# Adjacency visits of a graph kernel: three blocks take turns, and one operation marks the source rows of three visits

## What is computed

```python
def gnn_layer(x, W, b, src, dst):
    h = x @ W.T + b
    return relu(segment_sum(h[src], dst, num_segments=1250))

xn  = layernorm(x)
gnn = gnn_layer(gnn_layer(xn, W1, b1, src, dst), W2, b2, src, dst)
q, k, v = xn @ Wq.T, xn @ Wk.T, xn @ Wv.T
q = softmax(q, axis=-1) * 512 ** -0.5
k = softmax(k, axis=-2)                   # over the nodes
a = q @ (k.T @ v) + xn
x = x + gnn + (a @ M1.T @ M2.T + a)
x = x + moe(layernorm(x))                 # 8 experts, sinkhorn gates, 156 rows each
```

## Time and profile before

| | |
|---|---|
| median of 3 runs | 468.15 us (467.83 to 469.38) |
| the profiled execution | 468.61 us, of which 466.8 us are the span of its instructions |
| PE busy | 451.0 us, 97% of the span |
| DVE busy | 320.9 us, 69% |
| ACT busy | 150.6 us, 32% |
| granted clock of TensorE | 0.999 |
| stretch with visits (86 to 241 us) | PE busy all of it, DVE about nine tenths |

### The profile page before, as it was taken

One profiled execution on the slowest core, in us unless ns is written; L12 is line 12 of the kernel. 1 busy time (PEld: TensorE's weight loads), 2 busy tenths in 40 slices (PEclk: granted clock), 3 DMA queues, 4 the chain that ended last, 5 costly groups with the idle time before them and its releaser, 6 DMA issues.

```text
span 466.8 us, 6816 instructions
## 1 busy us (share of the span) xinstructions
PE 451.0 (97%) x2424; PEld 360.6 (77%) x2424; DVE 320.9 (69%) x1104; ACT 150.6 (32%) x272; POOL 63.1 (14%) x90
## 2 busy tenths in 40 slices
PE   7999999999999999999999999999999998878995
PEld 3788778888888888888779999877777776655783
DVE  6995699899998988897752110444645666777972
ACT  4686453322323332332222110222133114551110
POOL 4088200000000000000004000002300000006642
PEclk9999999999999999999999999999999999999999
DMA  8902002911000000001200000002744449305891
GB/s 219 287 1 91 1 0 91 219 50 65 2 1 1 1 1 1 1 2 20 108 0 4 1 1 1 1 0 53 277 139 134 134 142 380 131 1 190 289 356 71
DMA packets 20846, 40.46 MB, mean 87 GB/s; under 512 B 2953, under 2 KB 3283, under 8 KB 20805
## 3 DMA queue, kind: packets, MB, share of 16 engines
q1 hardware_dynamic: 18549, 32.55, 22.4%
q0 software_dynamic: 2256, 7.39, 4.5%
HBM read 30.10 MB, written 10.31 MB: 87 GB/s over the span
## 4 chain that ended last, share of the span: by engine, by line
PE 86%; DVE 8%; ACT 2%; issue 1%; DMA 1%; SPq 0%; POOLq 0%; DVEq 0%
PE ps L736 46%; PE ps L1031 9%; PE ps L957 9%; PE ps L848 5%; PE ps L723 5%; PE ps L1167 2%; ACT scrap_a L1424 1%; PE ps L1048 1%; PE ps L1137 1%; DMA X<-in_x 1%; PE ps L880 1%; PE ps L770 1%; PE ps L984 1%; PE ps L1008 1%; PE ps L1078 1%
## 5 line engine op out<-in xcount | busy, mean ns | idle before, releaser
L1713 DVE TENSOR_SCALAR RING_D<-places,PLACES 125x170 bf16<-125x170 f16 (+1 forms) x239 | 63.5, 266 | 0.0
L1714 DVE TENSOR_SCALAR RING_S<-iota,HOME 125x128 bf16<-125x128 f16 x239 | 60.4, 253 | 0.0
L957 PE MATMUL ps<-AT,H1H 125*128 125x416 f32 (+1 forms) x108 | 38.0, 352 | 0.0
L957 PE MATMUL ps<-AT,H1L 125*128 125x416 f32 (+1 forms) x108 | 38.0, 351 | 0.0
L1031 PE MATMUL ps<-H2H,AT 125*125 125x512 f32 x90 | 36.1, 402 | 0.0
L1031 PE MATMUL ps<-H2L,AT 125*125 125x512 f32 x90 | 35.5, 394 | 0.0
L1048 PE MATMUL ps<-WE0H 128*128 128x512 f32 x129 | 35.4, 408 | 0.0
L1781 DVE TENSOR_TENSOR ps<-ps,bias 125x512 f32<-125x512 f32 x20 | 14.0, 700 | 27.9 <-PE ps L736 27.9
L1860 DVE SCALAR_TENSOR_TENSOR ZL<-ps,ZH 128x416 fp32r<-128x416 f32 (+1 forms) x12 | 6.3, 585 | 38.7 <-ACT ZH L1369 38.7
L723 PEld LDWEIGHTS ps<-RING_D,RING_S 125*125 125x125 bf16 x239 | 25.7, 136 | 7.9
L605 POOL TENSOR_TENSOR G2L<-RAW_G,G2H 128x512 fp32r<-128x512 f32 x4 | 5.0, 1287 | 192.2 <-ACT G2H L1186 192.2
(11 more groups left out here) (410 smaller groups left out, 1171.7 us busy)
## 6 DMA issues: line engine op xcount, KB each, us to landing
RAW_E<-in_experts SPq DMA_DIRECT2D x8, 1024.0 KB, 9.9
RAW_AGAIN<-in_experts SPq DMA_DIRECT2D x3, 1024.0 KB
X<-in_x SPq DMA_DIRECT2D x1, 2240.0 KB
out_x<-X SPq DMA_DIRECT2D x10, 224.0 KB
scratch<-X SPq DMA_DIRECT2D x10, 224.0 KB
scratch<-Y SPq DMA_DIRECT2D x10, 224.0 KB
RAW_K<-in_WkT SPq DMA_DIRECT2D x4, 256.0 KB, 4.2
RAW<-in_mW2T SPq DMA_DIRECT2D x1, 1024.0 KB, 11.8
```

Source lines behind the costliest of these rows:

```text
L957: pe.matmul(place(f), h[0:TT, k, 128 * f:128 * (f + 1)], AT[0:TT, k, c0:c1], start=(k == 0 and n == 0), stop=False)
L1713: V.tensor_scalar(hot_d(v, width(b)), places[0:ET, 0:width(b)], PLACES[0:ET, c:c + 1], None, ALU.is_equal)
L1714: V.tensor_scalar(hot_s(v), iota[0:ET, :], HOME[0:ET, c:c + 1], None, ALU.is_equal).then_inc(done["marked"], 1)
```

## The change

The visits are regrouped in 104 **sets**: the 20 visits of block 0 in sets of up to 3, and then, inside a group, the visit number s of each of its blocks (block 0 apart) side by side. 87 sets hold 3 visits, 13 hold 2, 4 hold 1. For a set DVE still makes `hot_d` visit by visit, but all its `hot_s` in one operation: an equality of `iotas` (128 x 3, the row number written three times) with `HOME` of the set's visits, repeated over the 128 rows. The result is interleaved, so the weights of one visit lie 3 elements (6 bytes) apart. `HOME` becomes fp16. `marked` and `visited` count sets. Ring A holds 2 sets, ring B 9 sets. In PSUM a group is opened once, by its first matmul, and closed by its last.

The places change too: the places in vp and cp take one set each, `q{i}` has one place instead of two (2 sets), and `x{i}` has two, at 0 and 12, instead of four (3 sets each); 54 places in all. DVE's calls of `mark_next` are moved to match.

```diff
-RING_A, RING_B = 6, 16
+RING_A, RING_B = 2, 9
...
+    sets = [[(0, s) for s in range(o, min(o + SIDE, VISITS[0]))] for o in range(0, VISITS[0], SIDE)]
+    for g in range(NG):
+        blocks = range(max(SIDE * g, 1), min(SIDE * (g + 1), NB))
+        for s in range(VISITS[blocks[0]]):
+            sets.append([(b, s) for b in blocks if s < VISITS[b]])
...
-    spots = [("vp0", 6, 3)]
+    spots = [("vp0", 6, 1)]
     for u in ("vp1", "vp2", "vp3", "cp0", "cp1", "cp2", "cp3"):
-        spots += [(u, n, 3) for n in (0, 6)]
+        spots += [(u, n, 1) for n in (0, 6)]
     for i in range(NT + 1):
         if i < NT:
-            spots += [(f"q{i}", 0, 4), (f"q{i}", 6, 4 if i % 4 == 1 else 3)]
+            spots += [(f"q{i}", 0, 2)]
         if i:
-            spots += [(f"x{i - 1}", n, 3 if n == 12 else 4) for n in (0, 6, 12, 18)]
-    spots += [(f"h{i}", 6, 3) for i in range(NT)]
+            spots += [(f"x{i - 1}", n, 3) for n in (0, 12)]
+    spots += [(f"h{i}", 6, 1) for i in range(NT)]
...
-            link(nc.gpsimd.iota(iota[:], [[1, 128]], base=0, channel_multiplier=0,
+            link(nc.gpsimd.iota(iotas[:], [[1, 128], [0, SIDE]], base=0, channel_multiplier=0,
...
-                    pe.matmul(PS[4 + g % 2][0:TT, o:o + width(b)], hot_s(v)[:, 0:TT], hot_d(v, width(b)), start=(s == 0),
-                              stop=(s == VISITS[b] - 1), skip_group_check=True).then_inc(done["visited"], 1)
+                    for k, (b, s) in enumerate(SETS[v]):
+                        o = NT * (EDGES[b] - EDGES[SIDE * g])
+                        mm = pe.matmul(PS[4 + g % 2][0:TT, o:o + width(b)], hot_s(v)[:, 0:TT, k], hot_d(v)[:, k, 0:width(b)], start=(k == 0 and (b, s) == (SIDE * g, 0)),
+                                       stop=(v in GROUP_ENDS and k == len(SETS[v]) - 1), skip_group_check=True)
+                    mm.then_inc(done["visited"], 1)
...
-                        V.tensor_scalar(hot_d(v, width(b)), places[0:ET, 0:width(b)], PLACES[0:ET, c:c + 1], None, ALU.is_equal)
-                        V.tensor_scalar(hot_s(v), iota[0:ET, :], HOME[0:ET, c:c + 1], None, ALU.is_equal).then_inc(done["marked"], 1)
+                        for k, (b, _) in enumerate(SETS[v]):
+                            V.tensor_scalar(hot_d(v)[:, k, 0:width(b)], places[0:ET, 0:width(b)], PLACES[0:ET, c + k:c + k + 1], None, ALU.is_equal)
+                        V.tensor_tensor(hot_s(v)[:, :, 0:m], iotas[0:ET, :, 0:m], HOME[0:ET, c:c + m].unsqueeze(1).broadcast_to([ET, 128, m]),
+                                        ALU.is_equal).then_inc(done["marked"], 1)
...
             for c in range(C):
                 context_left(c)
-                mark_next(2)
+                mark_next((2, 2, 1, 2)[c])
             for i in range(NT + 1):
-                if i < NT and i:
+                if i:
                     mark_next()
                 if i >= 2:
                     add_mix(i - 2)
-                if i < NT and i:
-                    mark_next()
                 if i < NT:
                     q_peak(i)
                 if i:
-                    mark_next()
                     q_left(i - 1)
                     mark_next()
                 if i < NT:
                     q_inverse(i)
-                if i:
-                    mark_next()
+                if i and i < NT:
                     mark_next()
```

More of the change, by code:

```diff
@@ L188, with mark_sets @@
 EDGES, COLUMN = block_columns()
-ORDER = [(b, s) for b in range(NB) for s in range(VISITS[b])]
+def mark_sets():
+    sets = [[(0, s) for s in range(o, min(o + SIDE, VISITS[0]))] for o in range(0, VISITS[0], SIDE)]
[3 more added lines that the diff above has]
+            sets.append([(b, s) for b in blocks if s < VISITS[b]])
+    assert sum(map(len, sets)) == NV
+    for one in sets:
+        assert [COLUMN[x] for x in one] == list(range(COLUMN[one[0]], COLUMN[one[0]] + len(one)))
+    return sets
+SETS = mark_sets()
+NS = len(SETS)
+GROUP_ENDS = {v: SETS[v][0][0] // SIDE for v in range(NS) if v == NS - 1 or SETS[v + 1][0][0] // SIDE > SETS[v][0][0] // SIDE}
 def visits_in_products():
-    spots = [("vp0", 6, 3)]
+    spots = [("vp0", 6, 1)]
     for u in ("vp1", "vp2", "vp3", "cp0", "cp1", "cp2", "cp3"):
-        spots += [(u, n, 3) for n in (0, 6)]
+        spots += [(u, n, 1) for n in (0, 6)]
     for i in range(NT + 1):
         if i < NT:
-            spots += [(f"q{i}", 0, 4), (f"q{i}", 6, 4 if i % 4 == 1 else 3)]
+            spots += [(f"q{i}", 0, 2)]
         if i:
-            spots += [(f"x{i - 1}", n, 3 if n == 12 else 4) for n in (0, 6, 12, 18)]
-    spots += [(f"h{i}", 6, 3) for i in range(NT)]
+            spots += [(f"x{i - 1}", n, 3) for n in (0, 12)]
+    spots += [(f"h{i}", 6, 1) for i in range(NT)]
     found, v = [], 0
     for unit, n, count in spots:
-        count = min(count, NV - v)
+        count = min(count, NS - v)
         if count:
@@ L322, in gps_block @@
         tri = small("tri", [128, 128], F32, "a")
[L323 removed]
         places = small("places", [128, HOTW], F16, "a")
[L325 removed]
+        HOME = small("HOME", [128, NV], F16, "a")
         PLACES = small("PLACES", [128, NV], F32, "a")
@@ L346, in gps_block @@
         rsum = small("rsum", [128, 2, NT], F32, "a")
-        kmt = small("kmt", [128, C], F32, "a")
+        kmt = small("kmt", [128, C], F32, "k")
         krs = small("krs", [128, 2, C], F32, "a")
@@ L713, in visits @@
                 for v in VISITS_AT.get((unit, n), ()):
-                    b, s = ORDER[v]
-                    g = b // SIDE
-                    if s == 0 and b % SIDE == 0:
+                    g = SETS[v][0][0] // SIDE
+                    if SETS[v][0] == (SIDE * g, 0):
                         if g < 2:
```

41 lines of the change are left out of this document (22 added, 19 removed).

## The result

The changed kernel takes 472.34 us (median of 6 runs, 471.85 to 474.36) against 468.10 before (6 runs, 467.83 to 469.67): ratio 1.0086, 95% interval 1.0065 to 1.0107. It is slower by 4.2 us; the prediction said about 471.6 and "slower".

A forecast was written before the change was run, and what follows sets the result against it. PE sets the pace, DVE's savings alone are worth nothing. Transposes +0.82, moved visits +1.17, fewer places -1.03, loads +2.52 sum to +3.5 us: 472.1 profiled, about 471.6 median; whole range 467.3 to 476.5.

The forecast's parts named there:

- (a): PE's places for visits: 83 become 54, each costing 0.038 us of its own, so -1.1 us.
- (b): PE's weight loads in visits: 6-byte steps take 85 ns, +12 ns for each visit behind a visit, 2.8 us in all.
- one stream at 8.8 bytes/ns: Visits' weight load on PE: rate taken from the product's 512 fp32 columns, giving 85 ns for 750 bytes.
- the small prices of the earlier trace: PE loads of 128 weights: 0.046 us at 12-byte steps, 0.035 at 8; held perhaps not to carry over to 125.
- the load stays hidden: Rival for PE's visit loads: spaced weights cost nothing, +0.7 us, 468.9, no measurable difference; chance 0.27.
- as slow as fp32's: Rival for PE's visit loads: 107 ns each, 476.7 us in all; chance 0.08.
- (c): DVE's merged equality of 384 elements: 357 ns long, 0.265 us of DVE's time, a set of three 0.785.
- one element per cycle: Rival for DVE's set operation: 0.2 us more per set, +1.0 us on everything, 472.6 or 469.9; chance 0.10.
- (d): PE at tile 0's transposes: five sets in front of q_peak(0) delay the softmax, a wait of about 1.7 us.
- No other wait over 0.3 us in the stretch: PE in the stretch of the visits: besides 1 to 2 us idle once at L904, no wait above 0.3 us.
- disappears in the same wait: First visit of q1 on PE: perhaps 0.1 us late, absorbed by the wait at tile 0's transposes.

The follow-up runs named there:

- e9: Kernel before, on PE alone: the four places of each x run as two, visits of 0 in front of 6, 12 of 18; 468.30 us, ratio 1.0003.
- e1: Changed kernel with each home marked by itself into dense weights, sets, places and calls kept; 472.16 us, ratio 1.0083 to the kernel before.
- e2: Changed kernel with the three sets of the first place of x0 marked behind tile 0's softmax; 471.07 us, ratio 1.0062 to the kernel before.
- e7: Changed kernel with x0's first three sets marked behind tile 0's softmax, 128 weights a visit, two sets in h0; 469.43 us, ratio 1.0034.
- e11: e9 plus, in q2 to q9, the visits of place 0 run in front of matmul 6; 468.25 us, ratio 0.9994 to the kernel before.
- e12: e11 with DVE taking q_left(0) and q_left(9) one place earlier; 468.14 us against 468.88 for the kernel before, ratio 0.9987.
- b1: Changed kernel with rows of equal matmuls on PE and comparisons on DVE added to measure rates, results unused; 500.97 us in a single run.
- e8: Kernel before with 128 dense weights a visit instead of 125, nothing else; 469.53 us against 467.87, ratio 1.0041.

## Why the prediction was right, and where it was off

The forecast, about 471.6, stands 0.7 us below the measured 472.3, and the terms that make it up are the ones found; one is missing (below).

**(a) Fewer places.** Predicted 29 x 0.038 = 1.1 us. e9 gives 31 ns a place, so 0.9 us. The reason given, the next fp32 load that a visit is too short to hide, is what PE's loads show: the two fp32 loads behind a row of visits start 0.11 us apart (108 ns unrounded), the loads of visits 76, which is 32 ns more. In the kernel before, behind the four visits at 131.41:

```profile
131.63 0.19 PEld L736 LDWEIGHTS ps<-MPH,XTH 128*125 128x125 f32 x1
131.74 0.19 PEld L736 LDWEIGHTS ps<-MPL,XTH 128*125 128x125 f32 x1
```

The 38 were too much for two reasons. A visit behind a visit costs 75 ns, not 73 (by e1 and e9: 0.493 - 0.233 - 3 x 0.075 is 0.035). And the first visit of a row starts 229 ns behind the product's matmul, where the next matmul would start after 233, 4 ns that a count from the first visit on leaves out.

**(b) Weights 6 bytes apart.** Predicted 85 ns, measured 86.7 in the visits and 86 to 87.5 by itself. Against dense rows of the same length in e1, a row of nine is 0.090 longer, one of six 0.055, of three 0.018; over the 54 rows 2.6 us. The choice of "one stream at 8.8 bytes/ns" over the small prices of the earlier trace rows was the step that decided the sign, and half of it was luck. That those small prices don't carry over held: they are of 128 weights, which at 6 bytes take 33 ns or less. But the 8.8 bytes/ns came from a stream of columns, and the stream that was seen at both clocks hangs on the clock (170 columns: 144 ns at 0.50, 75 at 1.00), while the load doesn't. So the two are not the same thing, and that their rates are alike at a granted clock of 1.00 is luck as far as the runs show. The rival "the load stays hidden" is refuted, and so is "as slow as fp32's".

**(c) DVE's operation.** This is a mis-sized term: 0.357 us predicted and 0.265 of DVE's time; measured 0.423 and 0.334 (113.59 to 113.92). I took 0.5 ns an element from rows of 6 and 4, where pairs come out even; a row of three costs two pair steps. The rival "one element per cycle" (0.2 more) is wrong too; the truth is a third of the way.

**(d) The wait.** Predicted at the transposes of tile 0, 1.7 us; it is there and is 1.8. DVE's maximum came at 117.34, not 116.86: 5 x 0.07 of that is term (c), and 0.14 is that the five sets began at 113.07, not 112.93. e2 shows the mechanism by removing it: moving three sets behind the softmax takes the wait away and 1.7 us with it. `q1`'s first sets were late by 0.27 us (a row of six in 1.05 instead of 0.77), named at 0.1. "No other wait over 0.3 us in the stretch" held. That the small wait "disappears in the same wait" held as long as the large one stood; in e2, which has no large one, the late sets of `q1` count.

**Missed.** The places shift the last set from `h7` to `h8`, and PE loses 0.32 us between `h9` and the first matmul on `AT`. The prediction has no term for it: it counts the place, and not what waits behind the last group. e7 shows that it goes away when the last set stands in `h7` again.

The ledger in AT time: loads +2.6, wait at the transposes +1.8, wait in `q1` +0.3, last group +0.3, places -0.9: +4.1, measured +4.2. The prediction's was +3.5: the missing 0.7 are for the most part (c)'s 0.36 and the last group's 0.32; the smaller misses of (a), (b) and `q1` nearly cancel.

## What to carry to other kernels

When an operation on an engine with spare time is merged, look first at what its new output layout does to the engine that reads it: here 12 us less work on DVE bought nothing, and 6-byte steps in 125 bf16 weights cost PE 2.6 us. A weight load was free only while it was shorter than the stream in front of it: 57 ns vanish behind 170 columns at a pitch of 75, 86 don't. And a burst of preparatory work in front of a step that the critical engine will want soon is a wait, even if it is less work in sum; from e11 to e12 the placement of two steps was worth 0.7 us of AT time, nearly as much as all 28 places.

## What the runs showed of the hardware

- Loads of 125 bf16 weights take 57 ns dense, 60 at steps of 4 bytes, 86 at 6, 117 at 8, 173 at 12 and 226 to 229 at 16: from 6 bytes on 8.5 to 8.9 bytes/ns of distance walked, and at 16 bytes the same at the granted clocks 1.00 and 0.50 (b1). 128 weights take 33 ns or less, at 6 bytes too, and 46 at 12 (b1).
- Behind a matmul of the fp32 product, the load of 125 bf16 weights starts with that matmul, the load of 128 some 234 ns later; the first two bf16 matmuls come 9 and 9 ns (dense) or 9 and 18 ns (6 bytes) later. Behind fp32 transposes both loads start 2 ns behind the transpose. Loading more to get the faster load made the kernel before 1.4 us slower (e8). What holds the load back was not found out.
- Between a row of short bf16 matmuls and an fp32 product, the two fp32 loads behind the row start 108 ns apart, the bf16 ones 76. Each such place costs 31 ns (e9).
- In a two-source comparison on DVE with 16-bit data, a row of three costs two steps, as many as a row of four by the price of a step; an odd start costs nothing; 256 elements in rows of 2 and 128 in rows of 1 take the same (b1).
